# Graph attention on one core: the forward scan of the running maximum goes to PSUM, and the backward scan reads it there

## The reference, cut to what matters

```
score = einsum(leaky_relu(xl[src] + xr[dst]), att)        # 50000 edges x 8 heads
smax  = segment_max(score, dst)
ex    = exp(score - smax[dst])
out   = segment_sum(ex * xl[src], dst) / segment_sum(ex, dst)
```

## Time and profile before

| what | value |
|---|---|
| median of three runs | 2583.88 us (2580.75 to 2585.04) |
| span of the profiled execution, first to last instruction | 2587.6 us |
| TensorE busy | 2081.1 us (80%) |
| VectorE busy | 1677.9 us (65%) |
| GpSimd busy | 1666.0 us (64%) |
| ScalarE busy | 976.6 us (38%) |
| mean granted TensorE clock | 0.923 of full speed |

### The profile page before, as it was taken

The page is one execution under the profiler, slowest core; times in us unless marked ns, Lnnn a source line. Parts: engine busy times, 40 slices in busy tenths (PEclk is TensorE's granted clock), DMA queues, the critical chain, the costliest instruction groups (busy, mean ns, idle before and its releaser), DMA issues. The chain is left out here.

```text
span 2587.6 us, 31699 instructions
## 1 busy us (share of the span) xinstructions
PE 2081.1 (80%) x7770; PEld 1438.7 (56%) x7770; DVE 1677.9 (65%) x3422; ACT 976.6 (38%) x2578; POOL 1666.0 (64%) x1810
## 2 busy tenths in 40 slices
PE   1565655665499989799999999969699999999975
PEld 0443444444377765466666666645466666666654
DVE  9433222223266665488888888876488888888876
ACT  0121111111000013355555555544355555555543
POOL 3377777777400004788888888836788888888832
PEclk9777778778799999899999999989899999999987
DMA  3344353434498842544444444421544444444432
GB/s 95 85 121 116 119 116 120 116 120 116 124 268 262 264 125 77 131 113 112 113 125 112 113 112 113 108 64 47 126 110 114 113 114 112 113 113 112 112 74 99
DMA packets 208622, 311.81 MB, mean 120 GB/s; under 512 B 33396, under 2 KB 167542, under 8 KB 208471
## 3 DMA queue, kind: packets, MB, share of 16 engines
q0 software_dynamic: 64512, 171.82, 24.6%
q1 hardware_dynamic: 143799, 138.05, 20.6%
q10 hardware_dynamic: 160, 0.20, 0.0%
HBM read 243.75 MB, written 72.66 MB: 122 GB/s over the span
## 5 line engine op out<-in xcount | busy, mean ns | idle before, releaser
L1071 POOL DMA_INDIRECT gath<-gather_table,SRCI x880 | 849.7, 966 | 243.2 <-issue 209.4
L1121 PE MATMUL p_sums<-gath,OH 128*128 128x272 f32 x1760 | 477.2, 411 | 64.6 <-DVE gath L1028 29.3
L683 POOL DMA_INDIRECT rows_by_src<-gath,node x440 | 438.1, 996 | 138.0 <-issue 116.2
L627 PE MATMUL p_expd<-X,OHT 128*128 x880 | 296.8, 498 | 228.1 <-DVE OHT L589 213.1
L1090 PE MATMUL p_expd<-gath,ident 128*128 128x512 f32 x880 | 426.6, 608 | 33.1 <-DMA gath<-gather_table,SRCI 32.7
L1121 PEld LDWEIGHTS p_sums<-gath,OH 128*128 128x128 f32 x1760 | 323.9, 194 | 192.8 <-issue 89.7
L1094 PE MATMUL p_expd<-node,OHT 128*128 x1760 | 417.0, 380 | 0.0
L1094 PEld LDWEIGHTS p_expd<-node,OHT 128*128 128x128 f32 x1760 | 335.9, 191 | 141.6 <-issue 107.2
L627 PEld LDWEIGHTS p_expd<-X,OHT 128*128 128x128 f32 x880 | 210.0, 250 | 303.8 <-issue 267.3
L1149 DVE SCALAR_TENSOR_TENSOR work<-p_expd,VEC 128x512 f32<-128x512 f32 x440 | 282.0, 682 | 136.9 <-PE p_expd L1094 136.3
L1290 ACT ACTIVATE OH<-iota_row,NLOC 128x128 f32<-128x128 f32 x880 | 277.7, 386 | 8.1 <-PE p_sums L1121 8.0
(11 more groups left out here) (283 smaller groups left out, 2258.5 us busy)
## 6 DMA issues: line engine op xcount, KB each, us to landing
gath<-rows_by_src SPq DMA_DIRECT2D x122, 514.0 KB, 4.4
LBC<-local_rows SPq DMA_DIRECT2D x330, 128.0 KB, 3.0
gath<-gather_table,SRCI POOLq DMA_INDIRECT x880, 3.0
rows_by_src<-gath,node POOLq DMA_INDIRECT x440, 3.5
gather_table<-gath SPq DMA_DIRECT2D x50, 132.0 KB, 1.7
node<-gather_table SPq DMA_DIRECT2D x2, 3200.0 KB, 12.2
X<-in_x SPq DMA_DIRECT2D x1, 3072.0 KB
x<-X SPq DMA_DIRECT2D x5, 512.0 KB, 3.0
```

Of the source, the lines that this page charges most:

```text
L627: ins = pe.matmul(expd[q % 2][:, g // 2, (g % 2) * D:(g % 2 + 1) * D], OHT[:, q % 2, g * P:(g + 1) * P], Xv[:, bass.ds(tiles[g // 2], 1), ...
L683: pool.indirect_dma_start(sup_d[:, :], bass.IndirectOffsetOnAxis(POSI[:, i:i + 1], 0), U[:, q % 4, g, :], None, bounds_check=EP - 1, oob_i ...
L1071: pool.indirect_dma_start(ROWS[:, i % (RING * G), 0:XW], None, tab_d[:, :], bass.IndirectOffsetOnAxis(SRCI[:, i:i + 1], 0)).then_inc(gathe ...
L1121: ins = pe.matmul(sums[k][:, 0:RW], OH[:, a % 2, g, :], slots(a, g, g + 1)[:, 0, :], start=(g % 2 == 0), stop=(g % 2 == 1))
```

## The change

In `maximum` the forward scan writes to 128 unused columns of the PSUM bank `factors` (the new name `UPTO`) instead of the SBUF tensor FWD, and the backward scan reads them there. `ends` still uses FWD. Nothing else changes.

```diff
                 EXPS = factors[:, 0:P].rearrange("p (k h) -> p k h", h=H)
+                UPTO = factors[:, P:2 * P]
...
-                            link(dve.tensor_tensor_scan(FWD[:, 1:P + 1], RST[:, u, 0:P], BY_ROW, CR[:, 0:1], ALU.add, ALU.max))
-                            dve.tensor_tensor_scan(BWD[:, 0:P][:, ::-1], RST[:, u, 1:P + 1][:, ::-1], FWD[:, 1:P + 1][:, ::-1], CR[:, 1:2], ALU.add, ALU.max).then_inc(maxima, 1)
+                            link(dve.tensor_tensor_scan(UPTO, RST[:, u, 0:P], BY_ROW, CR[:, 0:1], ALU.add, ALU.max))
+                            dve.tensor_tensor_scan(BWD[:, 0:P][:, ::-1], RST[:, u, 1:P + 1][:, ::-1], UPTO[:, ::-1], CR[:, 1:2], ALU.add, ALU.max).then_inc(maxima, 1)
```

## The result

| | before | after |
|---|---|---|
| median of 15 runs each | 2581.48 us | 2577.29 us |
| lowest to highest | 2575.70 to 2586.91 | 2570.49 to 2582.72 |
| span of the profiled execution | 2587.6 us | 2577.1 us |
| its mean granted TensorE clock | 0.923 | 0.925 |
| VectorE busy | 1677.9 us | 1635.0 us |

The ratio is 0.998, 95% interval 0.9971 to 0.9989: the changed kernel is 0.2% faster, 5.2 us by the ratio (2.8 to 7.5). The prediction said 2575.1 us and a gain of 8.8. The sign and the place came out; the measured gain is six tenths of the forecast one (a third to 0.85 by the interval).

A forecast was written before the change was run, and what follows sets the result against it. GpSimd, which waits for nobody while gathers last, was taken to bound the edge loops. Taking 0.20 us off each of 46 gathers, 8.8 us as counted, brought the 2583.9 us median to 2575.1 us; range 2570 to 2586.

The forecast's parts named there:

- GpSimd sets the loops: In both edge loops GpSimd waits for nobody while gathers last, with 0.27 us before each gather; TensorE follows it.
- Backward scan 1.57 to 0.48, forward scan at no cost: In `maximum`, the backward scan saves 1.09 us per chunk, at most 61 us of VectorE time; the forward scan adds 0.
- The lead of `grow`, 0.43 us: In each chunk `grow` would be ready 0.43 us sooner, at 1158.21 instead of 1158.64, inside GpSimd's weighing.
- all further work of VectorE in this and the next step follows without a wait: After `shift`, VectorE runs on without waiting, so the 0.43 us gained there reaches `grow` whole.
- a lead of 0.05 is enough: Starting `grow` 0.05 us sooner would already put it inside GpSimd's weighing, so even 0.26 us would change nothing.
- `grow` queues and the gather is 0.98 behind it: `grow` waits for GpSimd's weighing, goes through 0.29 us behind it, and the next gather takes 0.98 us, not 1.18.
- The descriptors that wait for VectorE: At the gather behind `grow`: descriptors of a GpSimd-issued transfer wait for the port lock, held for VectorE's whole instruction.
- that of the 46 gathers: In the two loops, 23 gathers per layer each lose 0.20 us of excess, 8.8 us in all as counted.
- Nothing moves: Rival: the gather behind `grow` is held as before, or another two-SBUF operation meets a gather; 2583.9 us, chance 0.25.
- VectorE or TensorE is the path: Rival: another engine bounds the loops, saving 21 us (2563) or 61 us (2523); larger gains got chance 0.08.
- The scan is still blocked: Rival: the backward scan in `maximum` still waits for GpSimd, its operands and scalar staying in SBUF; 2583.9 us, chance 0.03.
- TensorE's clock: Rival: longer waits for GpSimd lower the loops' clock from 0.99 to 0.93, costing 40 us (2624); slower, chance 0.07.

The follow-up runs named there:

- the copy's run: Changed kernel plus a VectorE copy of GROW to PSUM, read by nobody, ahead of `grow`: 2721.07 us against 2720.54 for the kernel before, ratio 1.0001.
- the second batch: Runs on another chip, with the kernel before and the changed kernel repeated without edits: 2719.95 and 2713.35 us against 2720.54 for the kernel before.
- the change's second run: The changed kernel repeated without edits on another chip, against the kernel before there: 2713.35 us against 2720.54, ratio 0.9975.

## Why the prediction was right, and what in it was off

**GpSimd sets the loops: right.** The idle time before its gathers is unchanged at 0.27 us, the 42.9 us that VectorE's busy time fell by gave 5.2, and an instruction added to VectorE gave 7.0.

**Backward scan 1.57 to 0.48, forward scan at no cost: right.** 0.480 and 0.489 us. The backward scan with a PSUM source takes no more than the one with SBUF operands alone did where it wasn't blocked (0.483); the rule of the Trainium skill ("VectorE: DVE Perf Modes", section on the TRN2 errata) would have given an estimated 0.06 more, and the trace doesn't agree with it.

**The lead of `grow`, 0.43 us: wrong by half.** The step that failed is "all further work of VectorE in this and the next step follows without a wait". `shift` and its second half did start at once, but the product behind them did not. VectorE's own queue loads a register pair there, and the load, which formerly ran while the engine was busy, now stands in the open (start, length, instruction, of the trace's records for the queue and the engine; before, then after):

```
1153.683 0.593 TENSOR_LOAD L94              queue
1154.099 0.358 TENSOR_TENSOR L1194          shift
1154.574 0.678 SCALAR_TENSOR_TENSOR L1149   product

1150.066 0.369 TENSOR_TENSOR L1195          shift
1150.080 0.596 TENSOR_LOAD L94              queue
1150.723 0.691 SCALAR_TENSOR_TENSOR L1150   product
```

Before, the product started 0.475 behind `shift`; now 0.657, since it has to wait for the load's end at 1150.676. The product starts 0.05 behind that load in each of the 52 chunks of the changed kernel that have one. That takes 0.18 of the lead, and `grow` starts 0.92 us into the weighing and not 0.69; it lasts 0.44 us, not 0.6 to 0.7. The prediction was also wrong that a lead of 0.05 is enough. Since the gather ends 0.86 behind the end of `grow`, a `grow` 0.05 earlier than before would leave the gather at an estimated 1.12; for 0.99 it takes a lead of 0.18, and 0.20 arrived. Two chunks show how near that was: `grow` began 0.96 to 0.98 us into the weighing, and the gathers took 1.03 and 1.04. So that the whole gain came with less than half of the lead was luck, and the copy's run shows what lies beyond it.

**`grow` queues and the gather is 0.98 behind it: right, by its end and not by the queueing.** It was the riskiest step, argued from the blocked scan. In 42 chunks `grow` begins 0.29 to 0.32 us ahead of the gather, and the gather takes 0.99. A queued operation lets the gather go because it ends 0.29 behind the weighing, which is 0.13 behind the gather's start, while the gather ends 0.86 behind it as always. The Trainium skill ("SBUF — State Buffer", section "SBUF: two separate sides") has an operation that was admitted first hold the lock to its end. The gather that ends a constant 0.86 us behind a two-SBUF `grow`, queued or not, and the same gather at 0.98 when an operand is in PSUM, agree with it. The descriptors that wait for VectorE, which the prediction takes from the same section of the Trainium skill, wait there for an operation in a 2-port mode; of `tensor_tensor` the section says that it did not stall a DMA. Here `grow`, which is one, lengthened the instruction that issues the gather by 0.20 us, and the measurement decides.

**The sum: 8.8 us predicted, 5.2 measured (2.8 to 7.5).** The median, 2577.3 us, lies 2.2 above the forecast and inside its range. The term is that of the 46 gathers, 46 x 0.19, and it is mis-sized as a change of the total, not as a change of the loops: the profiled loops lost 9.7 us. (One of the 46, at 1068.19 us, was lengthened not by `grow` but by the backward scan of `ends`, L1166, begun 0.06 us ahead of it; it is gone after the change too.) In the second batch 6.8 (3.8 to 9.8) came out, with 42 collisions and 6.9 by the chunks' period. In the first comparison the interval leaves 8.8 out. In the profiled pair the stretch between the loops was 2.8 us longer, 2.1 of it in the first tail at its lower clock; but one pair can't separate that from the spread, since the untouched part ahead of the loops differs by 3.2 as well. Whether the tails give part of the gain back regularly there stays open.

**The rivals.** *Nothing moves* is ruled out by the timelines and by the interval; its worry about L1211 (L1212 now) was needless: it starts 0.05 behind the gather's start and leaves it at 0.99. Its mechanism, a gather that waits for the end of `grow`, is what the traces show; it costs 0.01 us where `grow` ends with the queue. *VectorE or TensorE is the path* fell: 0.45 us per chunk came free on TensorE and became 0.46 of waiting. *The scan is still blocked* fell with its 0.481 us maximum. *TensorE's clock* did not occur here, 0.99 before and after, but it can: with GpSimd out of the way the clock went to 0.83 and the time 15% up, an estimated half of it by slower matmuls.

## What to carry to other kernels

Find the engine that never waits, and look for the rows that break its rhythm; only what moves those is time, and a freed microsecond on another engine isn't. Where operations of two engines block each other, as `grow` and the gather do here, an edit upstream is worth what it does to the phase of an operation somewhere else, so its sign can turn with a shift of 0.2 us, and it is better to take one operand of the colliding operation out of SBUF than to rely on its place. And before relieving the pacing engine further, look at what it paces: the engine that sets the pace may be what keeps TensorE's work even and its clock up.

## What the runs showed of the hardware

- A VectorE operation with two SBUF operands that is blocked by a GpSimd operation ends 0.29 us behind it, whatever its own length (`grow` 0.44, the tail's 3.44, the backward scan in its 49 blocked cases of 56), and its record includes its wait.
- Of two 0.43 us operations with the same start, 0.1 us ahead of a gather, the one with two SBUF operands lengthens the gather by 0.20 us and the one with an operand in PSUM by nothing. The gather ends 0.85 to 0.86 us behind the end of the first (211 cases in five profiles).
- The load of registers at L94 on VectorE's queue takes 0.59 to 0.60 us in the chunks shown. It is hidden as long as the engine has work, and delays the next instruction, here the product by 0.18 us, when the engine has caught up.
- Taking 0.44 us per group from the engine that sets the pace (5.98 to 5.54) went with a fall of the mean clock between 1200 and 1750 us from 1.00, in the change's second run, to 0.83, and a kernel 15% slower; with 0.33 us of idle work in each group (5.91 us) the clock was 1.00 and the ratio 0.9960.
